# A DMA turns the rounded pairs where TensorE transposed them, in a two-product kernel on one core

## What is computed

```python
selected_W = W[cat_ids]                                   # by element
c = jnp.einsum('bsd,bdh->bsh', x, selected_W) + b[cat_ids][:, None, :]
w_scale = jnp.mean(jnp.abs(weight)) + EPS
w_quant = jnp.clip(jnp.round(weight / w_scale), -1.0, 1.0)
a_scale = jnp.max(jnp.abs(c), axis=-1, keepdims=True) + EPS
a_quant = jnp.round(jnp.clip(c / a_scale * 127.0, -128.0, 127.0))
y = jnp.einsum('bsi,oi->bso', a_quant, w_quant) * (w_scale * a_scale / 127.0)
return x + y
```

## Time and profile before

| | us |
|---|---|
| median of 3 runs | 504.2 (503.44 to 505.55) |
| the profiled execution | 504.57 |
| its span, first to last instruction | 502.8 |
| PE busy | 490.8 |
| DVE, ACT, POOL busy | 369.0, 335.1, 304.2 |

### The profile page before, as it was taken

One profiled execution on the slowest core, in us unless ns is written; L12 is line 12 of the kernel. 1 busy time (PEld: TensorE's weight loads), 2 busy tenths in 40 slices (PEclk: granted clock), 3 DMA queues, 4 the chain that ended last, 5 costly groups with the idle time before them and its releaser, 6 DMA issues. The chain is left out here.

```text
span 502.8 us, 13149 instructions
## 1 busy us (share of the span) xinstructions
PE 490.8 (98%) x2215; PEld 359.4 (71%) x2216; DVE 369.0 (73%) x653; ACT 335.1 (67%) x503; POOL 304.2 (60%) x398
## 2 busy tenths in 40 slices
PE   7889999999999999999999999999999999999996
PEld 2667777777777776777777776777777677777774
DVE  5668686487966797988766879865988587566844
ACT  3667765677667667768656686766768667467642
POOL 7686575565765755765755656565655665665650
PEclk9999999999999999999999999999999999999999
DMA  6779998999989999999999899999999999799953
GB/s 229 259 231 413 412 319 298 361 379 372 391 283 392 379 410 414 409 383 404 349 303 357 299 406 411 405 314 325 413 381 394 368 365 351 252 365 338 317 165 126
DMA packets 71874, 172.75 MB, mean 344 GB/s; under 512 B 8114, under 2 KB 8498, under 8 KB 71730
## 3 DMA queue, kind: packets, MB, share of 16 engines
q1 hardware_dynamic: 54002, 140.07, 76.1%
q10 hardware_dynamic: 17856, 32.51, 17.3%
HBM read 139.00 MB, written 33.55 MB: 343 GB/s over the span
## 5 line engine op out<-in xcount | busy, mean ns | idle before, releaser
L355 POOL TENSOR_TENSOR sb_xT_lo<-sb_xT_raw,sb_xT_hi 128x512 fp32r<-128x512 f32 x128 | 190.6, 1489 | 167.7 <-PE ps_cond L718 166.6
L716 PE MATMUL ps_cond<-sb_w_hi,sb_xT_hi 128*128 (+1 forms) x512 | 224.7, 439 | 3.5 <-POOL sb_xT_lo L355 1.6
L718 PE MATMUL ps_cond<-sb_w_hi,sb_xT_lo 128*128 (+1 forms) x512 | 201.3, 393 | 0.0
L717 PE MATMUL ps_cond<-sb_w_lo,sb_xT_hi 128*128 (+1 forms) x512 | 199.4, 390 | 0.0
L613 DVE TENSOR_REDUCE sb_absmax<-ps_cond 128x1 f32<-128x512 f32 x128 | 87.9, 686 | 110.3 <-PE ps_cond L718 106.4
L567 DVE TENSOR_TENSOR sb_w_lo<-sb_w_raw,sb_w_hi x106 | 143.6, 1393 | 0.0
L400 ACT ACTIVATE ps_cond<-sb_w_raw 128x512 f32 x127 | 75.7, 596 | 88.1 <-issue 56.9
L680 PE MATMUL ps_y<-sb_ffnT,sb_aT 128*128 128x512 bf16 x508 | 130.1, 379 | 1.0 <-ACT sb_aT L467 0.9
L486 ACT ACTIVATE sb_a_rounded<-ps_cond,sb_a_inv 128x512 int8<-128x512 f32 x128 | 87.7, 685 | 52.1 <-DVE sb_a_inv L619 51.7
L716 PEld LDWEIGHTS ps_cond<-sb_w_hi,sb_xT_hi 128*128 128x128 f32 x512 | 96.3, 188 | 36.2 <-issue 6.7
L718 PEld LDWEIGHTS ps_cond<-sb_w_hi,sb_xT_lo 128*128 128x128 f32 x512 | 96.0, 188 | 22.4
(11 more groups left out here) (83 smaller groups left out, 47.4 us busy)
## 6 DMA issues: line engine op xcount, KB each, us to landing
sb_w_raw<-cond_wb SPq DMA_DIRECT2D x53, 768.0 KB, 7.5
sb_xT_raw<-x_t SPq DMA_DIRECT2D x128, 256.0 KB, 5.7
sb_x_rows<-x SPq DMA_DIRECT2D x128, 256.0 KB, 5.8
out<-sb_x_rows ACTq DMA_DIRECT2D x124, 256.0 KB, 5.7
sb_w_raw<-cond_wb SPq DMA_DIRECT2D x53, 512.0 KB, 5.6
sb_w_raw<-cond_wb SPq DMA_DIRECT2D x5, 256.0 KB, 4.3
sb_ffn_raw<-ffn_t SPq DMA_DIRECT2D x1, 1024.0 KB, 5.6
out<-sb_x_rows SPq DMA_DIRECT2D x3, 256.0 KB, 2.3
```

The lines of the kernel that those rows point to most:

```text
L355: pool.tensor_tensor(xT_lo[:, m, :], xT_raw[:, m, :], xT_hi[:, m, :].bitcast(F32), ALU.subtract).then_inc(x_lo_done, 1)
L716: pe.matmul(ps_cond, x_hi_k, w_hi_k, start=(start and k == 0), stop=False, skip_group_check=True)
L717: pe.matmul(ps_cond, x_hi_k, w_lo_k, start=False, stop=False, skip_group_check=True)
L718: last_mm = pe.matmul(ps_cond, x_lo_k, w_hi_k, start=False, stop=(k == KD - 1), skip_group_check=True)
```

## The change

The transpose leaves TensorE. SP issues a transposing DMA (`dma_start_transpose`) that reads the 128 x 512 int8 of `a_rounded` as 128 x 256 pairs of two bytes and writes them, turned in two blocks of 128 columns, into a new SBUF tile `a_pairs`. ACT's move reads `a_pairs` and takes the two bytes of each pair apart. The host orders the rows of the second weight to match. The PSUM banks of the transposes go to the second product, which has four now.

In the bodies: SP's step r begins with the turn of step r-1, behind waits on the move four steps earlier and on the rounding, and ahead of its loads. The move is 4 steps behind (2 before), the second product 5 (3), the store 6 (4); the rows of x are loaded for step r-2 instead of r+1. ACT's wait for the transpose, ahead of its rounding, falls away. `y_scale` gets eight places. PE's end has five second products behind the last first product where it had three.

```diff
-    COND_BANKS, PS_RING = 4, 2
-    LO_AHEAD, HI_AHEAD, W_AHEAD, XT_AHEAD, ROWS_AHEAD = 3, 4, 6, 5, 1
-    X_AHEAD, SEED_AHEAD, T_BEHIND, Y_BEHIND, STORE_BEHIND = 2, 3, 2, 3, 4
+    COND_BANKS, PS_RING = 4, 4
+    LO_AHEAD, HI_AHEAD, W_AHEAD, XT_AHEAD = 3, 4, 6, 5
+    X_AHEAD, SEED_AHEAD, T_BEHIND, MOVE_BEHIND, Y_BEHIND, STORE_BEHIND, ROWS_BEHIND = 2, 3, 1, 4, 5, 6, 2
...
+        a_pairs = sb("a_pairs", [P, Q_RING, H], I8)
...
-        y_scale = sb("y_scale", [P, STAT_RING])
+        y_scale = sb("y_scale", [P, U])
...
-        aT_ps = [ps(f"aT{n}") for n in range(PS_RING)]
...
+            def transpose_pairs(step, n):
+                q = n % Q_RING
+                sp.wait_ge(a_rounded_done, step + 1)
+                sp.sem_inc(rounded_taken, 1)
+                sp.dma_start_transpose(a_pairs[:, q, :].bitcast(I16).rearrange("p (b s) -> p b s", s=S),
+                                       a_rounded[:, q, :].bitcast(I16)).then_inc(pairs_landed[q], 16)
...
                 row = row_of(sp, r + W_AHEAD, NEW, ROWS_ELEMENT + 1)
+                if not first or u >= T_BEHIND:
+                    if not first or u - T_BEHIND >= Q_RING:
+
+                        sp.wait_ge(aT_moved, r - T_BEHIND - Q_RING + 1)
+                        sp.sem_inc(pairs_freed, 1)
+                    transpose_pairs(r - T_BEHIND, (u - T_BEHIND) % U)
...
-                if not last or u + ROWS_AHEAD < U:
-                    n = (u + ROWS_AHEAD) % U
-                    if not first or u + ROWS_AHEAD >= U:
-                        sp.wait_ge(stored[n], rows_landed(r + ROWS_AHEAD - U, n))
+                if not first or u >= ROWS_BEHIND:
+                    n = (u - ROWS_BEHIND) % U
+                    if not first:
+                        sp.wait_ge(stored[n], rows_landed(r - ROWS_BEHIND - U, n))
                     load_rows(bounded(sp, row[ROWS_ELEMENT], B - 1), n)
...
+            for step in range(B - ROWS_BEHIND, B):
+                (element,) = row_of(sp, step + W_AHEAD + ROWS_BEHIND, ROWS_ELEMENT, 1)
+                sp.wait_ge(stored[step % U], rows_landed(step - U, step % U))
+                load_rows(bounded(sp, element, B - 1), step % U)
+            for step in range(B - T_BEHIND, B):
+                sp.wait_ge(aT_moved, step - Q_RING + 1)
+                transpose_pairs(step, step % U)
...
             def move(step, n, first):
 
-                act.wait_ge(aT_done, step + 1)
+                act.wait_ge(pairs_landed[n % Q_RING], pairs_there(step, n % Q_RING))
                 if not first or n >= Q_RING:
                     act.wait_ge(y_mm_done, step - Q_RING + 1)
-                packed = aT_ps[n % PS_RING][:, 0:P].bitcast(I8)
-                act.activation(aT[:, n % Q_RING, :].rearrange("p (k s) -> p k s", k=KH),
-                               packed.rearrange("p (s k) -> p k s", k=KH), ACT.Copy).then_inc(aT_moved, 1)
+                act.activation(aT[:, n % Q_RING, :].rearrange("p (b t s) -> p b t s", t=2, s=S),
+                               a_pairs[:, n % Q_RING, :].rearrange("p (b s t) -> p b t s", t=2, s=S),
+                               ACT.Copy).then_inc(aT_moved, 1)
...
-                if not first or u >= T_BEHIND:
-                    move(r - T_BEHIND, (u - T_BEHIND) % U, first)
-                if not first or u >= Q_RING:
-                    act.wait_ge(aT_done, r - Q_RING + 1)
+                if not first or u >= MOVE_BEHIND:
+                    move(r - MOVE_BEHIND, (u - MOVE_BEHIND) % U, first)
...
-            def a_transpose(step, n, first):
-                pe.wait_ge(a_rounded_done, step + 1)
...
-                if not first or u >= T_BEHIND:
-                    a_transpose(r - T_BEHIND, (u - T_BEHIND) % U, first)
                 if not first or u >= Y_BEHIND:
                     second_product(r - Y_BEHIND, (u - Y_BEHIND) % U, first)
                 if last and u == U - 1:
-                    a_transpose(r - 1, u - 1, False)
-                    second_product(r - 2, u - 2, False)
-                    a_transpose(r, u, False)
-
-                    second_product(r - 1, u - 1, False)
+                    for behind in range(Y_BEHIND - 1, 0, -1):
+                        second_product(r - behind, u - behind, False)
...
-    ffn_rows = ffn.T.reshape(P, H // P * O)
+    ffn_rows = ffn.T.reshape(H // (2 * P), P, 2, O).transpose(1, 0, 2, 3).reshape(P, H // P * O)
```

More of the change, by code:

```diff
@@ L9 @@
 I8 = mybir.dt.int8
+I16 = mybir.dt.int16
 ALU = mybir.AluOpType
@@ L96, in adaln_ffn @@
         raw_offset_col = sb("raw_offset_col", [P, 1], BF16)
-        table = sb("table", [1, B + W_AHEAD, COLUMNS], I32)
+        table = sb("table", [1, B + W_AHEAD + ROWS_BEHIND, COLUMNS], I32)
         act_table = sb("act_table", [1, B + HI_AHEAD + STORE_BEHIND, HI_COLUMNS], I32)
@@ L130, in adaln_ffn @@
         w_half_loaded = [sem(f"w_half_loaded{n}") for n in range(U)]
+        pairs_landed = [sem(f"pairs_landed{n}") for n in range(Q_RING)]
         stored = [sem(f"stored{n}") for n in range(U)]
@@ L171, in adaln_ffn @@
         a_rounded_done = sem("a_rounded_done")
-        aT_done = sem("aT_done")
+        rounded_taken = sem("rounded_taken")
+        pairs_freed = sem("pairs_freed")
         aT_moved = sem("aT_moved")
@@ L215, in rows_landed, with pairs_there @@
             return (step - n) * (16 // U) + 16
+        def pairs_there(step, n):
+            return (step - n) * (16 // Q_RING) + 16
         def w_landed(step, n):
@@ L272, in _ @@
             sp.dma_start(ffn_raw[:, :], ffn_t[:, :]).then_inc(ffn_loaded, 16)
-            sp.dma_start(x_rows[:, 0, :], x[0, :, :]).then_inc(rows_loaded[0], 16)
+            def transpose_pairs(step, n):
[4 more added lines that the diff above has]
+                                       a_rounded[:, q, :].bitcast(I16)).then_inc(pairs_landed[q], 16)
             def xT_of(row):
@@ L379, in body @@
                 pool.sem_inc(absmax_taken, 1)
-                pool.tensor_scalar(y_scale[:, s:s + 1], absmax[:, s:s + 1], EPS, w_step[:, 0:1],
+                pool.tensor_scalar(y_scale[:, u:u + 1], absmax[:, s:s + 1], EPS, w_step[:, 0:1],
                                    ALU.add, ALU.mult).then_inc(y_scale_done, 1)
@@ L428, in _ @@
             act.wait_ge(elements_mm_done, 1)
-            for column, behind in ((XT_ELEMENT, W_AHEAD - XT_AHEAD), (ROWS_ELEMENT, W_AHEAD - ROWS_AHEAD)):
+            for column, behind in ((XT_ELEMENT, W_AHEAD - XT_AHEAD), (ROWS_ELEMENT, W_AHEAD + ROWS_BEHIND)):
                 act.activation(table[:, behind:behind + B, column], y_ps[1][0:1, 0:B],
@@ L490, in body @@
                 if last and u == U - 1:
-                    for n in range(U - T_BEHIND, U):
+                    for n in range(U - MOVE_BEHIND, U):
                         move(B - U + n, n, False)
@@ L594, in result @@
             def result(step, n):
-                s = n % STAT_RING
                 dve.wait_ge(y_mm_done, step + 1)
@@ L598, in result @@
                 dve.wait_ge(rows_loaded[n], rows_landed(step, n))
-                dve.scalar_tensor_tensor(x_rows[:, n, :], y_ps[n % PS_RING][:, :], y_scale[:, s:s + 1],
+                dve.scalar_tensor_tensor(x_rows[:, n, :], y_ps[n % PS_RING][:, :], y_scale[:, n:n + 1],
                                          x_rows[:, n, :], ALU.mult, ALU.add).then_inc(y_done, 1)
@@ L636, in _ @@
             dve.wait_ge(rows_loaded[U - 1], rows_landed(B - 1, U - 1))
-            s = (B - 1) % STAT_RING
+            s = U - 1
             for half in range(2):
```

## The result

| | before | after |
|---|---|---|
| median of 5 runs, us | 504.2 (503.44 to 505.55) | 614.77 (609.68 to 615.47) |
| the profiled execution, us | 504.57 | 609.68 |
| its span, us | 502.8 | 607.9 |

The changed kernel takes 1.2157 times as long, 95% interval 1.2119 to 1.2196: 110.6 us more, where 8 were forecast, and beyond the end of the range at 592. The direction was right, the size was not, and the resource that sets the end is one to which the forecast gave nothing: SyncE.

The account below looks back on a forecast made before the run. PE was taken to bound the kernel on average, DMA in full stretches. From 504.57 us, +5.8 for slices, -0.3 for the tail and +2.5 for stalls gave 512.6, put at 512 us for the median; range 498 to 592.

Parts of the forecast that it names:

- value: nothing: SP's queue: its mean step rises from 2.84 to 3.4 us, below PE's 3.62, so it adds no time.
- SP bound: Rival on SP's queue: issuing a turn takes 0.9 us or more, SP needs 3.94 us a step, 531 us; chance 0.08.
- a DMA price of over 1 us: Rival in the DMA engines: small pieces hold them 0.7 to 1.3 us a step, 536 to 603 us; chance 0.22.
- DMA price: DMA engines: each turn takes 0.35 us of their time, twice the plain price of 0.175 us.
- the forecast's +5.8 us: Sum over time slices of the larger of PE and DMA time: full DMA slices lose 10.5 us, PE-bound ones gain.
- nets out: Rival in the DMA engines: at 0.2 to 0.3 us a step gain and cost cancel, 502 to 506 us; chance 0.13.
- the forecast 3.62: PE's step: without the transpose it falls from 3.73 to 3.62 us, a gain of at most 13.9 us.
- no cost at all: Low end of the faster rival: the turn is free in the DMA engines, 490 us; rival's chance 0.17 (490 to 501).
- slice formula: Each 12.57 us slice costs the larger of PE time, 12.2 us, and DMA time including 0.35 us per turn.
- the allowance of three steps: ACT's move wants the turn three steps, 10.9 us, after its issue; enough in the mean, not behind two weight loads.
- -0.3: Kernel's end: the last turn's path adds 1.4 us, two more second products running beside it save 1.7.
- my signs: Expected in the trace: PE steps of 3.62 us, DMA share 1.0 or above, ACT waiting for pairs, turn issue near 0.33 us.

Follow-up runs that it names:

- the plain copy's 524 us: The changed kernel with the turn replaced by a plain DMA of the same 64 KB on SP's queue: 524.43 us, 1.0369 times before.
- the run of three reads: The kernel before, with SyncE reading its table row three times a step, each read used, and no byte more: 619.88 us, 1.2244 times before.
- the run without a turn: The changed kernel without the turn's DMA; SP raises the semaphore itself and ACT's move reads a constant tile: 502.28 us, 0.9936 times before.
- the plain copy from ScalarE: The changed kernel with the turn's issue moved to ScalarE and the turn made a plain copy of the same 64 KB: 508.34 us, 1.0056 times before.

## Why the prediction was wrong

**SP, "value: nothing": the step that failed.** I priced the issue of the turn at 0.33 us because the issues of weights and of x, of quite different rows, take 0.35 and 0.33 us. Those rows differ in size, but both are plain copies; they could say nothing of another kind of DMA. It measured 1.19 us. The trace of before had no such operation. I bounded the engines' time for it from both sides, but gave the issue the price of a plain DMA and left the rest to a rival. The second half of the failure needs no turn. I put SP's mean at 2.84 us from one step of each kind and the surroundings of the issue at about 0.2 us. They are 2.97 and 0.42. With a plain issue (0.48 us) SP is at 3.90, above the 3.62 that I allowed: the plain copy's 524 us. A slack of 0.2 us of 3.62 was no ground for "nothing".

**The rival "SP bound"** named the mechanism and its point of decision (0.9 us), with 0.08 of the chance. Its term was mis-sized too: 2.84 + 0.2 + 0.9 = 3.94 us and 531 us, where 2.97 + 0.42 + 1.22 = 4.61 us was measured. With the same addition, 18 + 128 x 4.61, it would have been 608. The range ended at 592 for quite another reason (a DMA price of over 1 us).

**DMA price: about right, and off the path.** I took 0.35 us per turn. Compared with the run of three reads, which is as slow and has no turn, q1 took 77.2% of 607.9 = 469.3 us against 67.6% of 619.7 = 418.9: 0.39 us a step. By ScalarE's queue, against the run without a turn, it is 0.35 (24.3% of 528.1 us and 16.7% of 502.2), and a plain copy there 0.22. Such shares are rough: the same packets took q1 382.6 us in the kernel before and 418.9 with three reads, and against the run without a turn the price on SP's queue would come out at 0.68. The Trainium skill, Advanced Engine Details and Errata, section "X-Bar Transpose (TRN2)", has transposing DMAs as fast as regular ones; here 64 KB took 0.35 us where the plain copy took 0.22, so the trace disagrees. That the engines' price stands near where I put it did not matter: the time of a DMA on its issuer is another term than its time in the engines. The full stretches at 404 to 414 GB/s, from which the forecast's +5.8 us came, no longer occur once SP issues late. Whether 512 us would hold with a free issue wasn't tried, as no issue is free; the plain copy from ScalarE, at 508.34 us, is near the case "nets out" (502 to 506).

**PE: the step was right, its worth was not.** L691 is gone, and L704 follows the last L732 by 0.22 to 0.23 us where it need not wait (589.93 to 590.16). The step at best is 3.647 us against the forecast 3.62. But the rival "no cost at all" at 490 us was out of reach: 502.28 measured. My own slice formula, with no price for the turn, would have given the ten full slices next to nothing and so some 11 us; I took 13.9 as if every step were bound by PE.

**ACT.** The move is 614 ns, between the bounds 583 and 629. It waited 4.5 us in all for pairs, in two waits at the very end, so the allowance of three steps was enough: landings are 4.4 us in the median, 8.5 at most.

**Tail, "-0.3": it was +5.9.** Between the end of the last rounding and the last step's second product it was 1.75 us; now it is 6.9 (595.81 to 602.69). I counted an issue of 0.4, a landing of 2.1 and the move. SP still had to issue three loads of rows and then the turn, 1.19 us, from 598.67 on:

```profile
595.03 1.19 SPq L285 DMA_TRANSPOSE sb_a_pairs<-sb_a_rounded  x1
596.41 2.12 SPq L241 DMA_DIRECT2D sb_x_rows<-x  x3
598.67 1.19 SPq L285 DMA_TRANSPOSE sb_a_pairs<-sb_a_rounded  x1
```

The first conditioning matmul is at 12.43 us (12.76 before), the last high-by-high one at 593.13 (493.97), the end of the span at 607.9 (502.8). So 99.5 us of the 105.1 are in the steps and 5.9 behind them.

**What would have shown it.** Of my signs, "SP: issue of the turn near 0.33 us" failed, and it names the cause. Two others failed as well: the DMA share was to stand at 1.0 or above and was 0.96, and ACT was to show waits for the turned pairs and had two, at the end. PE's idle time did grow, from 5 to 66 us between 20 and 460 us, but 45 of these were on the move (L704 on L493) and only 8 on x_lo, seeds and w_lo. Idle time that grows fits both causes, and so do falling GB/s. Signs that both causes share don't tell them apart; SP's list of waits, empty here where it had 89 us in 430 before, does.

## What to carry to other kernels

A DMA has two prices, one in the engines and one on the queue that issues it; for another kind of DMA the second must be bounded like the first, and set against the issuer's mean step, with everything that it does between issues. When all engines wait, look for the one that doesn't: a queue without waits is the bound, even where its instructions count as no busy time in the page. To test that, load that queue with work that moves no byte.

## What the runs showed of the hardware

- A transposing DMA of 128 x 256 two-byte values held its issuing queue for 1.19 us on SyncE and 1.23 on ScalarE; of 128 x 128 values 1.12; a plain copy of the same 64 KB 0.48; plain loads 0.33 to 0.42. The Trainium skill, DMA: Bandwidth & Descriptors, section "Issuing engines are not separate DMA queues", calls the issuing time that another queue saves usually small relative to the DMA. Here it was not: the same DMAs, issued by ScalarE, took 86 of 615 us less.
- The 128 turns brought 36,864 packets below 512 B more than before, 288 for each turn; half a turn brought 160, a plain copy of the same bytes 16. The changed kernel stood at a busy share of 0.96 with 307 GB/s, the kernel before at 0.98 with 361. A share near 1 told nothing of how much more could be moved.
- TensorE's granted clock was 0.96 of the 2.4 GHz level between 20 and 460 us after the change, and 0.96 in the run of three reads, which has no turn; before it was 1.00. In the timeline after the change conditioning matmuls are 0.23 us apart up to 302.8 us; TensorE then stands idle for 2.3 us ahead of the next second product, and from 307.6 to 310.1 they are 0.43 us apart, the level of 1.2 GHz. It is a consequence and not the cause: in neither kernel did SP wait for others in the loop, so SP set the pace in both.
- Reading six values of a table into registers cost SP 0.8 to 0.9 us in the mean, over twice a plain load's issue. Two more such reads cost 115 us.
